# A new order of the opening of a cross-attention and LoRA-expert kernel, and a last tile stored in three parts

## What is computed

```python
# block 1: attention of every row to 64 context rows of its batch
scores = einsum('bsd,bmd->bsm', layernorm(x), ctx) / sqrt(1024)
attn = softmax(where(mask, scores, -1e30))
x = x + where(any(mask), einsum('bsm,bmd->bsd', attn, ctx), 0)
# block 2: a dense layer and the two best of 8 rank-16 experts
y = layernorm(x)
base = y @ weight.T                      # 1024 -> 1024
w_dense = top-2 of softmax(y @ router_w.T), renormalised
x = x + base + 2 * einsum('nd,erd->ner', y, lora_A) * w_dense @ lora_B
```

## Time and profile before

| | us |
|---|---|
| time, median of 3 runs (1094.65 to 1096.60) | 1096.17 |
| time of the profiled execution | 1095.92 |
| its span, first to last instruction | 1094.1 |
| TensorE busy with matmuls | 1074.6 |
| VectorE busy | 789.2 |
| ScalarE busy | 466.5 |
| GpSimd busy | 114.2 |

### The profile page before, as it was taken

One profiled execution on the slowest core, in us unless ns is written; L12 is line 12 of the kernel. 1 busy time (PEld: TensorE's weight loads), 2 busy tenths in 40 slices (PEclk: granted clock), 3 DMA queues, 4 the chain that ended last, 5 costly groups with the idle time before them and its releaser, 6 DMA issues.

```text
span 1094.1 us, 18329 instructions
## 1 busy us (share of the span) xinstructions
PE 1074.6 (98%) x6240; PEld 1045.9 (96%) x6240; DVE 789.2 (72%) x2047; ACT 466.5 (43%) x954; POOL 114.2 (10%) x282
## 2 busy tenths in 40 slices
PE   7899999999999999999999999999999999999998
PEld 6799999999999999999999999999999999999998
DVE  5867867768677777677777677677776677776663
ACT  5643443443443443443533444434444434434330
POOL 2510010010010010110000100100100100100100
PEclk8999999999999999999999999999999999999999
DMA  9453534643535543544536434445435635345322
GB/s 323 112 164 116 154 84 129 183 136 116 153 81 161 153 123 127 142 115 137 153 105 173 129 95 142 134 147 151 117 95 153 163 116 154 78 133 154 92 64 78
DMA packets 70974, 145.89 MB, mean 133 GB/s; under 512 B 8848, under 2 KB 44176, under 8 KB 70928
## 3 DMA queue, kind: packets, MB, share of 16 engines
q1 hardware_dynamic: 70496, 143.78, 45.6%
q10 hardware_dynamic: 432, 1.57, 0.4%
HBM read 78.74 MB, written 33.55 MB: 103 GB/s over the span
## 4 chain that ended last, share of the span: by engine, by line
DVE 44%; issue 18%; ACT 16%; PE 13%; POOL 7%; DMA 1%; ACTq 1%; POOLq 0%; SPq 0%; DVEq 0%
DVE x2T L698 10%; DVE x L680 7%; DVE stats L686 7%; DVE xT_lo L705 6%; DVE xT_lo L647 6%; ACT xT_hi L451 4%; PE base_ps L836 4%; PE base_ps L838 4%; PE base_ps L837 4%; POOL rstd L384 3%; ACT x2T L437 3%; ACT xT_hi L481 3%; ACT e_all L463 2%; POOL rstd L380 1%; ACT e_split L465 1%
## 5 line engine op out<-in xcount | busy, mean ns | idle before, releaser
L836 PE MATMUL base_ps<-w_hi,xT_hi 128*128 128x388 f32 x1512 | 529.9, 350 | 2.6 <-DVE x L750 1.2
L837 PE MATMUL base_ps<-w_lo,xT_hi 128*128 128x388 f32 x1512 | 511.9, 339 | 0.0
L838 PE MATMUL base_ps<-w_hi,xT_lo 128*128 128x388 f32 x1512 | 511.7, 338 | 0.0
L836 PEld LDWEIGHTS base_ps<-w_hi,xT_hi 128*128 128x128 f32 x1512 | 285.2, 189 | 14.6 <-DVE x L750 4.4
L837 PEld LDWEIGHTS base_ps<-w_lo,xT_hi 128*128 128x128 f32 x1512 | 285.1, 189 | 2.7
L838 PEld LDWEIGHTS base_ps<-w_hi,xT_lo 128*128 128x128 f32 x1512 | 284.2, 188 | 0.0
L475 ACT ACTIVATE xn<-x,shift,rstd 128x1024 f32<-128x1024 f32 x63 | 78.4, 1245 | 313.7 <-POOL shift L387 313.7
L481 ACT CAST xT_hi<-x2T 128x512 fp32r<-128x512 f32 x126 | 72.0, 618 | 129.5 <-DVE x2T L698 129.5
L698 DVE STREAM_TRANSPOSE x2T<-xq 128x512 f32<-128x512 f32 x126 | 126.6, 1081 | 0.0
L384 POOL TENSOR_TENSOR rstd<-var_eps,neg_half 128x1 f32<-128x1 f32 x64 | 36.0, 563 | 688.6 <-DVE var_eps L691 688.6
L705 DVE TENSOR_TENSOR xT_lo<-x2T,xT_hi 128x512 fp32r<-128x512 f32 x126 | 81.4, 687 | 34.8 <-ACT xT_hi L481 34.8
(11 more groups left out here) (98 smaller groups left out, 1159.8 us busy)
## 6 DMA issues: line engine op xcount, KB each, us to landing
out<-x SPq DMA_DIRECT2D x64, 512.0 KB, 3.9
x<-in_x SPq DMA_DIRECT2D x63, 512.0 KB, 3.4
xq<-xn SPq DMA_DIRECT2D x252, 128.0 KB, 3.5
xT_raw<-in_xT SPq DMA_DIRECT2D x62, 512.0 KB, 5.2
ctx_raw<-in_ctx SPq DMA_DIRECT2D x16, 256.0 KB, 5.3
w_raw<-in_wT SPq DMA_DIRECT2D x8, 386.0 KB, 8.2
ctxT_raw<-in_ctxT SPq DMA_DIRECT2D x8, 256.0 KB, 4.6
w_raw<-in_wT SPq DMA_DIRECT2D x4, 388.0 KB, 9.6
```

The costliest lines, as they stand in the source:

```text
L836: pe.matmul(out_, a_hi, w_h, start=start, stop=False, skip_group_check=again)
L837: pe.matmul(out_, a_hi, w_l, start=False, stop=False, skip_group_check=again)
L838: return pe.matmul(out_, a_lo, w_h, start=False, stop=stop, skip_group_check=again)
```

## The change

Nothing of the arithmetic changes. The schedule does, in the opening and at the last tile:

- SyncE: `ctxT` of batch 0 comes in two halves, one from SyncE and one from ScalarE; the mask is loaded ahead of the context; ScalarE's queue loads `xT` of tile 1 before tile 1. `load_xT((0, 4))` comes before the exchange of tile 1.
- TensorE: `first_scores(1)` directly behind tile 0's; the readout of tile 0 first uses the high part of the context in both halves and then the low part; other numbers of `warm`; the readout of tile 1 within and behind group 0; `pair_scores((0, 2))` behind two products of group 2; tile 2's `e_transpose` and `readout` now in group 0 of tile 1.
- ScalarE: tile 0's normalised rows in two halves, each with a semaphore; the casts of the weight parts in another order among the rest; the high part of `bT` moves here from GpSimd.
- GpSimd and VectorE: `ctx_low(0)` moves from VectorE to GpSimd; the low parts of the weights are shared out otherwise; tile 2's softmax comes behind tile 1's block transposes, `add_bases((0, 0))` ahead of tile 2's `add_readout`.
- The last tile: `h_transpose` after two chunks, groups 0 and 1 are finished with their `lora_second` before the last two chunks of group 2, and the tile is stored by three DMAs, one for each group.

```diff
@@ sync
-            load_ctxT(0)
+            sp.dma_start(ctxT_raw[:, 0:HC, :], ctxT_in[0][:, 0:HC, :]).then_inc(ctxT_loaded, 16)
             sp.dma_start(x[:, 0, :], x_in[0]).then_inc(x_loaded[0], 16)
+            load_mask(0)
             load_ctx(0)
...
-            exchange((0, 1))
             sp.wait_ge(xT_split, 2)
             load_xT((0, 4))
+            exchange((0, 1))
...
+            for g in range(G):
+                o0, n = OUTS[g]
+                sp.wait_ge(out_done, count(LAST, G, FREE + g + 1))
+                sp.dma_start(out[NT - 1][:, o0:o0 + n], x[:, slot(LAST), o0:o0 + n]).then_inc(stored[slot(LAST)], 16)
@@ gpsimd
             norm1((0, 0))
-            pool.wait_ge(softmax_step, 2)
-            norm1((0, 1))
-            w_low(pool, 0, 0)
+            ctx_low(pool, 0)
+            pool.wait_ge(e_split_done, 1)
+            w_low(pool, 0, 1)
             norm2((0, 0))
             w_low(pool, 0, 2)
-            w_low(pool, 1, 0)
+            norm1((0, 1))
+            w_low(pool, 0, 3)
             w_low(pool, 1, 1)
+            w_low(pool, 1, 2)
             norm2((0, 1))
-            w_low(pool, 1, 2)
-            w_low(pool, 1, 3)
             w_low(pool, 2, 0)
             w_low(pool, 2, 1)
-            pool.wait_ge(b_loaded, 16)
-            pool.tensor_copy(b_hi[:, :], b_raw).then_inc(b_hi_done, 1)
@@ scalar
+            act.dma_start(ctxT_raw[:, HC:C, :], ctxT_in[0][:, HC:C, :]).then_inc(second_half_loaded, 16)
             act.dma_start(xT_raw[:, 0, 0], xT_in[0]).then_inc(xT_loaded[0][0], 16)
+            act.dma_start(xT_raw[:, 0, 1], xT_in[1]).then_inc(xT_loaded[0][1], 16)
             act.dma_start(x[:, 1, :], x_in[1]).then_inc(x_loaded[1], 16)
-            act.dma_start(xT_raw[:, 0, 1], xT_in[1]).then_inc(xT_loaded[0][1], 16)
             xT_high((0, 0), 0)
+            norm1_mean((0, 0))
             ctxT_high(0)
-            norm1_mean((0, 0))
             norm1_squares((0, 0))
+            xT_high((0, 0), 1)
+            ctx_high(0)
             first_sT_copy()
-            ctx_high(0)
+            w_high(0, 0)
             softmax_exp((0, 0))
-            xT_high((0, 0), 1)
             eT_copy((0, 0))
-            for r in range(3):
+            second_sT_copy()
+            for r in range(1, WPARTS):
                 w_high(0, r)
-            second_sT_copy()
-            w_high(0, 3)
+            for r in range(2):
+                w_high(1, r)
             first_norm2()
+            first_x2T_high()
             softmax_exp((0, 1))
-            first_x2T_high()
+            for r in range(2, WPARTS):
+                w_high(1, r)
             eT_copy((0, 1))
-            for r in range(WPARTS):
-                w_high(1, r)
             for i in range(2):
                 xT_high((0, 2), i)
+            for r in range(2):
+                w_high(2, r)
             norm2((0, 1))
             gate_exp((0, 0))
-            for r in range(WPARTS):
+            for r in range(2, WPARTS):
                 w_high(2, r)
-            sT_copy((0, 2))
+            b_high()
             norm1_mean((0, 2))
             norm1_squares((0, 2))
+            sT_copy((0, 2))
+            hT_high((0, 0))
+            x2T_high((0, 1))
             softmax_exp((0, 2))
...
@@ vector
             mask(0)
-            first_norm1_stats()
+            xT_low((0, 0), 1)
             softmax_scores((0, 0))
-            ctx_low(0)
             softmax_split((0, 0))
-            xT_low((0, 0), 1)
+            w_low(dve, 0, 0)
             add_readout((0, 0))
             norm2_stats((0, 0))
+            first_norm1_stats()
+            first_x2T_low()
             softmax_scores((0, 1))
-            w_low(dve, 0, 1)
             softmax_split((0, 1))
-            first_x2T_low()
-            w_low(dve, 0, 3)
+            w_low(dve, 1, 0)
             add_readout((0, 1))
             norm2_stats((0, 1))
-            for i in range(2):
-                xT_low((0, 2), i)
+            w_low(dve, 1, 3)
+            xT_low((0, 2), 0)
             router_top((0, 0))
             router_gate((0, 0))
+            xT_low((0, 2), 1)
             w_low(dve, 2, 2)
             w_low(dve, 2, 3)
-            softmax_scores((0, 2))
             b_low()
-            softmax_split((0, 2))
             hT_low((0, 0))
+            dve.wait_ge(ln1_step, count((0, 2), 2, 2))
             for i in range(TS):
                 x2_transposes((0, 1), i)
             x2T_low((0, 1))
-            xT_low((0, 4), 0)
+            softmax_scores((0, 2))
+            softmax_split((0, 2))
+            add_bases((0, 0))
             add_readout((0, 2))
             norm2_stats((0, 2))
-            add_bases((0, 0))
+            xT_low((0, 4), 0)
@@ tensor
             warm(5)
             ctx_mean(0)
-            warm(6)
+            warm(5)
             pe.wait_ge(ctxT_split, 1)
             first_scores(0)
             pe.wait_ge(first_sT_copied, 1)
             pe.transpose(st_ps, sT[:, 0:P], ident[:, :]).then_inc(scores_done, 1)
-            warm(8)
-            e_transpose((0, 0))
-            readout((0, 0))
             first_scores(1)
             warm(1)
+            e_transpose((0, 0))
+            first_readout()
+            warm(4)
             scores((0, 1))
-            warm(8)
+            warm(12)
             first_x2_transposes()
+            first_base(0, 0, range(C))
+            first_base(0, 1, range(C))
+            first_base(0, 2, range(HC))
             e_transpose((0, 1))
-            first_base(0, 0)
+            first_base(0, 2, range(HC, C))
             readout((0, 1))
-            first_base(0, 1)
-            first_base(0, 2)
             for product in range(3):
-                first_base(1, product)
+                first_base(1, product, range(C))
+            for product in range(2):
+                first_base(2, product, range(C))
             pair_scores((0, 2))
-            first_base(2, 0)
+            first_base(2, 2, range(HC))
             scores((0, 2))
-            first_base(2, 1)
             h_transpose((0, 0))
-            first_base(2, 2)
+            first_base(2, 2, range(HC, C))
+            for g in range(G):
+                lora_second((0, 0), g)
+            base((0, 1), 0, range(HC))
             e_transpose((0, 2))
-            lora_second((0, 0), 0)
-            lora_second((0, 0), 1)
+            base((0, 1), 0, range(HC, C))
             readout((0, 2))
-            lora_second((0, 0), 2)
-            for j in range(1, TPB):
+            rest((0, 1))
+            for j in range(2, TPB):
                 step((0, j))
...
+            base(LAST, 0, range(C))
+            base(LAST, 1, range(C))
+            base(LAST, 2, range(2))
+            h_transpose(LAST)
+            base(LAST, 2, range(2, 6))
+            lora_second(LAST, 0)
+            lora_second(LAST, 1)
+            base(LAST, 2, range(6, C))
+            lora_second(LAST, 2)
```

More of the change, by code:

```diff
@@ L282, in w_low, with ctx_low @@
                                  ALU.subtract).then_inc(w_split[g][r], 1)
+        def ctx_low(engine, b):
+            engine.wait_ge(ctx_hi_done, b + 1)
+            engine.tensor_tensor(ctx_lo[:, :], ctx_raw[:, :], ctx_hi[:, :].bitcast(f32),
+                                 ALU.subtract).then_inc(ctx_split, 1)
         @block.sync
@@ L356, in _ @@
                     step((b, j))
-            for j in range(TPB):
+            for j in range(TPB - 1):
                 step((NB - 1, j))
+            for g in range(G):
+                o0, n = OUTS[g]
+                sp.wait_ge(out_done, count(LAST, G, FREE + g + 1))
+                sp.dma_start(out[NT - 1][:, o0:o0 + n], x[:, slot(LAST), o0:o0 + n]).then_inc(stored[slot(LAST)], 16)
             for s in range(XS):
-                sp.wait_ge(stored[s], 16 * NT // XS)
+                sp.wait_ge(stored[s], 16 * NT // XS + (16 * (G - 1) if s == slot(LAST) else 0))
         @block.gpsimd
@@ L502, in first_norm2 @@
                 act.wait_ge(shift2_done, 1)
-                act.activation(xn[:, :].rearrange("p (c a n) -> p a c n", a=Q, n=QP),
-                               x[:, 0, :].rearrange("p (a c n) -> p a c n", a=Q, n=QP), ACT.Identity,
-                               bias=shift2[:, :], scale=rstd2[:, :]).then_inc(xn_done, 1)
+                for i, done in enumerate([first_xn_half, xn_done]):
+                    act.activation(half(xn, i).rearrange("p (c a n) -> p a c n", a=Q, n=QP),
+                                   x[:, 0, :].rearrange("p (a c n) -> p a c n", a=Q, n=QP)[:, :, i * HC:(i + 1) * HC],
+                                   ACT.Identity, bias=shift2[:, :], scale=rstd2[:, :]).then_inc(done, 1)
             def first_x2T_high():
@@ L511, in first_x2T_high, with b_high @@
                     act.copy(chunks(xT2_hi[:, 0], i), base_bank((0, 0), 1 + i)[:, :]).then_inc(x2T_hi_done, 1)
+            def b_high():
+                act.wait_ge(b_loaded, 16)
+                act.copy(b_hi[:, :], b_raw).then_inc(b_hi_done, 1)
```

(25 more changed lines are left out.)

17 lines of the change are left out of this document (9 added, 8 removed).

## The result

The changed kernel is **slower**: 1102.25 us (median of 4 runs, 1101.52 to 1102.65) against 1095.49 for the kernel before beside it, a ratio of 1.006 with a 95% interval of 1.0043 to 1.0078. The profiled execution took 1102.33 us with a span of 1100.6, 6.5 more than before. Forecast were 1093.6 us and, as the slow end of the range, 1097.5. The runs of one kernel spread by 2 to 3 us (28 runs of the kernel before: 1093.1 to 1096.7), so in what follows a difference of one microsecond is read from marks in the traces, and each trace is one execution.

The account below looks back on a forecast made before the run. TensorE, busy 1074.6 of 1094.1 us, was taken as the bound, so only the opening and the end could give: 1.85 + 0.75 = 2.6 us, 1096.17 - 2.6 = 1093.6 us. The range was 1090.3 to 1097.5.

Follow-up runs that it names:

- e2_gate_first: Changed kernel with tile 1's router gate and tile 3's first norm ahead of tile 2's second norm: 1101.67 us, 1.0058 to the kernel before.
- e1_fill_pause: Changed kernel with 14 useless matmuls ahead of the transpose of h of tile 1: 1100.99 us, 1.0048 to the kernel before.
- e4_xTlow_later: Changed kernel with VectorE's low part of tile 4's first half behind the gate of tile 1, not ahead of its router: 1103.47 us, 1.0068 to the kernel before.

## What to carry to other kernels

When a part is moved behind other work, follow the longest chain that starts at it, not the first engine that waits: here 16 us from a readout to the next tile's first matmul, of which a reordering nearer its end (`e2_gate_first`) gave back 1.1 us, and the move of the readout itself 5.3. Where two engines share a port, small instructions of one placed in a dense run of the other's long ones can cost up to one long instruction each (1.19 and 1.63 us instead of 0.23 and 0.16); a single wait that lets them through gave 0.9 us, where the new loads alone gave nothing. Look at what the clock does behind every pause that an edit makes, moves or shortens: here it took back what earlier casts had gained, and gave 1.4 us to an edit that was meant for something else. And bring one early load forward only with the name of the load that it delays.

## What the runs showed of the hardware

A granted clock of 1.00 ahead of the first change that a trace holds can be wrong: in the changed kernel the windows say 1.00 from 10 to 20 us, while score matmuls of 128 columns follow each other at 0.21 us. In `e1_fill_pause`, the same program up to there, they follow each other at 0.21 us, too, and the windows say 0.50 from 11 to 24. The distance of equal matmuls is the surer reading in the first microseconds:

```profile
10.24 0.41 PE L873 MATMUL s_ps<-xT_hi,ctxT 128*128 128x128 f32 x1
10.45 0.41 PE L874 MATMUL s_ps<-xT_lo,ctxT 128*128 128x128 f32 x1
```

How long the clock stays low varies, even for the same program. A wait of 3.8 us in which TensorE stood was followed by the low clock for 7 us (changed kernel), one of 2.8 us at nearly the same place for 10 (`e4_xTlow_later`); filled with useless matmuls, it was followed by none. The pause of 2.0 us at 40 us was followed by 3.4 us of low clock in the changed kernel and by 6.9 in `e1_fill_pause`, with 1.1 us lost by it at tile 1's group 0.
